# Latent attention in a 16-head kernel: the query product and its rotation issued behind all three score groups of a head

## What is computed

```python
qc = rms_norm(x @ wq_down, q_norm_w)                  # 96 columns
q_nope = (qc @ wq_up).reshape(bs, seq_len, H, DN)     # 16 heads
q_pe = apply_rope((qc @ wq_rope).reshape(bs, seq_len, H, DR), cos, sin)
kvc = rms_norm(x @ wkv_down, kv_norm_w)               # 64 columns
scores = jnp.einsum('bqhd,bkhd->bhqk', q, k) * scale  # causal mask
probs = softmax(scores + mask)
out = jnp.einsum('bhqk,bkhd->bqhd', probs, v).reshape(bs, seq_len, H * DV)
return out @ wo
```

## Time and profile before

| what | value |
|---|---|
| three runs | 1478.59, 1483.33, 1485.69 us; median 1483.33 |
| the profiled execution, its own time | 1489.86 us |
| its span in the trace | 1487.8 us |
| TensorE busy | 1288.7 us (87%) |
| VectorE busy | 949.1 us (64%) |
| ScalarE busy | 672.6 us (45%) |
| GpSimd busy | 493.0 us (33%) |
| mean granted TensorE clock | 0.945 of full speed |

### The profile page before, as it was taken

The page is one execution under the profiler, slowest core; times in us unless marked ns, Lnnn a source line. Parts: engine busy times, 40 slices in busy tenths (PEclk is TensorE's granted clock), DMA queues, the critical chain, the costliest instruction groups (busy, mean ns, idle before and its releaser), DMA issues.

```text
span 1487.8 us, 22532 instructions
## 1 busy us (share of the span) xinstructions
PE 1288.7 (87%) x6702; PEld 831.9 (56%) x6702; DVE 949.1 (64%) x2798; ACT 672.6 (45%) x1706; POOL 493.0 (33%) x495
## 2 busy tenths in 40 slices
PE   6769898898887599998769889889889997899997
PEld 4514243343335588887536455556556555778886
DVE  6786758777778322224598878887897793033334
ACT  2205655565672055553245444554554452255550
POOL 2054040052214455551211211351143143355551
PEclk7959998999999799999998999999999998899999
DMA  8627543074304276544010000020010112255647
GB/s 284 107 27 114 184 85 43 1 147 152 146 25 159 96 240 196 189 153 143 15 43 29 29 1 1 11 103 1 8 37 15 58 36 100 94 198 180 207 136 300
DMA packets 78928, 152.15 MB, mean 102 GB/s; under 512 B 11677, under 2 KB 60254, under 8 KB 75230
## 3 DMA queue, kind: packets, MB, share of 16 engines
q1 hardware_dynamic: 63022, 108.59, 25.5%
q0 software_dynamic: 15360, 41.96, 7.9%
q10 hardware_dynamic: 432, 0.17, 0.0%
HBM read 85.29 MB, written 65.01 MB: 101 GB/s over the span
## 4 chain that ended last, share of the span: by engine, by line
PE 56%; DVE 28%; ACT 6%; issue 6%; DMA 3%; POOL 1%; SPq 0%; DVEq 0%; POOLq 0%; ACTq 0%
PE m_psG L1263 12%; PE m_psY L1279 5%; DVE a_t L1713 5%; DVE a_mx L914 4%; PE a_psA L1472 3%; DVE a_nb L1721 3%; PE a_psO L478 3%; PE m_psX L1254 3%; PE a_psU L1454 3%; PE a_psU L453 3%; ACT a_pr L1583 2%; PE m_psY L161 2%; PE a_psO L1495 2%; PE a_psW L419 2%; PE a_psP L1485 2%
## 5 line engine op out<-in xcount | busy, mean ns | idle before, releaser
L166 POOL DMA_INDIRECT outs_dram<-m_ys,dest x192 | 183.9, 958 | 166.4 <-ACT m_ys L1184 152.5
L1583 ACT ACTIVATE a_pr<-a_psA,a_nb 128x512 f32<-128x512 f32 (+3 forms) x256 | 132.6, 524 | 220.2 <-DVE a_nb L1721 219.3
L1204 DVE TENSOR_TENSOR m_hm<-m_psG,m_sg 128x128 f32<-128x128 f32 x192 | 56.0, 292 | 270.1 <-ACT m_sg L1178 171.2
L1263 PE MATMUL m_psG<-arena,m_xgT 128*128 x768 | 203.6, 388 | 3.9 <-ACT m_xgT L1172 2.7
L914 DVE TENSOR_REDUCE a_mx<-a_psU 128x1 f32<-128x512 f32 x256 | 163.6, 684 | 67.5 <-PE a_psU L453 61.7
L1639 POOL TENSOR_TENSOR a_q<-a_q,a_t 64x512 f32<-64x512 f32 x64 | 80.8, 1263 | 356.5 <-DVEq L1716 336.1
L166 POOL DMA_INDIRECT rows_dram<-a_xd,slot x112 | 115.0, 1027 | 157.0 <-DVE a_xd L146 74.5
L602 ACT ACTIVATE a_P<-a_psS 128x512 f32<-128x512 f32 x256 | 142.8, 597 | 51.1 <-PE a_psS L464 44.9
L1263 PEld LDWEIGHTS m_psG<-arena,m_xgT 128*128 128x128 f32 x768 | 131.6, 191 | 20.8 <-issue 9.2
L1721 DVE TENSOR_REDUCE a_nb<-a_psA 128x1 f32<-128x512 f32 (+3 forms) x256 | 113.3, 485 | 38.1 <-PE a_psA L1474 28.5
L453 PE MATMUL a_psU<-arena 96*128 96x512 bf16 x256 | 106.1, 416 | 33.2 <-DVE a_mx L914 31.2
(11 more groups left out here) (296 smaller groups left out, 2377.4 us busy)
## 6 DMA issues: line engine op xcount, KB each, us to landing
m_xg<-rows_dram SPq DMA_DIRECT2D x46, 512.0 KB
arena<-in_mo_w SPq DMA_DIRECT2D x9, 2048.0 KB
arena<-part_dram SPq DMA_DIRECT2D x96, 128.0 KB
arena<-outs_dram SPq DMA_DIRECT2D x18, 512.0 KB, 3.9
rows_dram<-a_P SPq DMA_DIRECT2D x6, 1024.0 KB, 14.2
part_dram<-a_part SPq DMA_DIRECT2D x16, 384.0 KB, 5.4
rows_dram<-arena SPq DMA_DIRECT2D x6, 1024.0 KB, 15.0
arena<-outs_dram SPq DMA_DIRECT2D x5, 1024.0 KB, 11.1
```

Of the source, the lines that this page charges most:

```text
L166: pool.indirect_dma_start(out=rows_dram, out_offset=bass.IndirectOffsetOnAxis(ap=slot[:, c:c + 1], axis=0), in_=row, in_offset=None).then_ ...
L1263: ins = pe.matmul(psG[b % 2][:, 0:2 * INTER], xgT[:, (b % 2) * D + k * P:(b % 2) * D + (k + 1) * P], GU[:, ds(e * (KD * 2 * INTER) + k * 2 ...
L1583: ins = act.activation(pr[S % 2][:, AT[t]:AT[t] + (t + 1) * P], psA[:, AT[t]:AT[t] + (t + 1) * P], ACT.Exp, bias=nb[S % 2][:, t:t + 1], sc ...
```

## The change

Two loops are reordered and nothing else. TensorE issues all three groups of scores of head S and then the query product of head S + 2. VectorE takes all three groups of maxima and then rotates that query. The unit order in `psU`, the semaphores, the other engines' lists and all shapes stay.

```diff
@@ TensorE, step S @@
                 if S < HEADS:
-                    scores(S, 0)
+                    for k in range(NBK):
+                        scores(S, k)
                     if S + 2 < HEADS:
                         queries(S + 2)
-                    for k in range(1, NBK):
-                        scores(S, k)
                 if S >= 3 and S % 2:
                     values((S - 3) // 2)
@@ VectorE, step S @@
-                maxima(S, 0)
+                for k in range(NBK):
+                    maxima(S, k)
                 if S + 2 < HEADS:
                     queries(S + 2)
-                for k in range(1, NBK):
-                    maxima(S, k)
                 for k in range(NBK):
                     divide(S, k)
```

## The result

The changed kernel takes 1543.05 us (median of 4 runs, 1541.75 to 1548.56) beside 1484.51 us for the kernel before on the same chip: 1.0392 times, with a 95% interval of 1.0363 to 1.0422, so **58.5 us slower**. The forecast was 1526, with 1507 to 1547 as its range.

A forecast was written before the change was run, and what follows sets the result against it. VectorE and TensorE were both taken as near full, each pacing some latent-stage steps. Step costs, less 2.9 us of returns, plus 3.4 for the clock, summed to +42.4 us on 1483.3: 1525.7, say 1526, range 1507 to 1547.

The forecast's parts named there:

- the clock rival: Longer pauses before every side unit put TensorE's half clock on further steps: about 1543, up to 1555 us; chance 0.14.
- signs of being wrong: First division product near 0.5, steps without side unit at 5.87 or less, or steps growing with clock well below 0.96.
- The collision: GpSimd's addition holds VectorE's first division product: 0.91 us lost, net +0.69 a VectorE-paced step, 12.4 over 18 steps.
- the savings: On VectorE, taking the maxima together removes gaps and overlaps the rest: 0.22 us saved in a VectorE-paced step.
- Steps entered with TensorE last: Seven steps ended by VectorE, where the query product now comes later on TensorE: +1.28 us each, 9.0 in all.
- Steps 14, 16, 32 and 48: These four steps were counted at 4.0 us in the sum.
- Scatter steps: Nine steps where stores make GpSimd late: -0.22 to +0.69 us each, taken as 0.45, 4.0 in all.
- Even output products: TensorE's output products wait for the later rotation: 4.5 us (20, 36, 52), 3.2 (18, 34, 50), clock 3.4 (34, 50).
- Steps 9, 25 and 40: Steps 9 and 25 at +0.3 us, step 40 at +1.0: 1.6 in all.
- The returns from earlier exponentials: Earlier ScalarE exponentials give back time in steps 13 (-1.5), 15 (-0.75), 31 and 47 (-0.3): -2.9 us in all.
- no collision: GpSimd's addition starts late enough to slip between VectorE's products: +9.1 us, 1492; chance 0.12.
- earlier exponentials free TensorE: TensorE's 21.9 us of score waits on ScalarE go, with the collision absent: 1461 us; chance 0.04.

The follow-up runs named there:

- the filler run: The full change plus 12 filler products of 128x128 on TensorE ahead of every side unit of an even step: 1526.36 us, 1.0265 times the kernel before.
- the collision alone: The kernel before, order untouched, but GpSimd's addition waits for the last maximum so that it starts with the division: 1504.55 us, 1.0188.
- the run without most of the collisions: The full change, with GpSimd's addition waiting for the next head's first maximum except in steps that also scatter rows: 1510.52 us, 1.0162.
- the 18 chosen steps: The kernel before, with the new order and GpSimd's addition behind the next first maximum only in 18 VectorE-paced steps: 1484.72 us, 1.0000.

## Why the prediction was right, and what it missed

The direction and the main cause were right, and the time is inside the range. It is 17 us above the forecast, though, and on the very number of the clock rival (about 1543); one of my own signs of being wrong came as well, the clock row at 0.91, well below 0.96. That the range reached to 1547 is what covers this. Measured 58.5 us against 42.4: the terms, summed over the steps of the two traces (56.1 us there):

- *The collision.* Worked out: product ends 0.28 behind the addition, +0.69 a VectorE-paced step, 6.56. Measured: 0.29, +0.79 in the plain ones, 6.64 to 6.66, and the 18 steps named together 13.5 for 12.4. The step of the working that was short is the hand-over from the last product of the division to the first maximum of the next step: I let it start 0.08 before the product's end, as in the old order, and it starts 0.03 behind it (1009.67 in step 33 without the collision, where the product ends at 1009.64). So the savings were 0.13 instead of 0.22, and that step takes 5.74, not 5.65. Why the overlap is gone I have not found.
- *Steps entered with TensorE last:* 1.30 to 1.86 each for 1.28; 10.2 for 9.0. Steps 14, 16, 32 and 48: 4.5 for 4.0. Step 0: 1.1 for 2.2. Even key steps: 1.7 for 1.0.
- *Scatter steps:* 6.9 for 4.0, of which step 29 alone 2.9.
- *Even output products:* 14.6 for 11.1, clock included. I left step 20 at full clock (10.3); it took 12.14. Steps 36 and 52 did come at 10.45.
- *Steps 9, 25 and 40:* 4.1 for 1.6.
- *The returns from earlier exponentials* are **the term that failed**: -2.9 was counted, -0.6 came (13: 0.0, 15: -0.2, 31: -0.2, 47: -0.2). The exponentials did come earlier, but steps 13 and 15 lost the gain again: 13 takes 8.10, with a granted clock of 0.79, 6.67 with the fillers, and 6.44 with the addition beside the next maxima, where 15 takes 6.45 for 7.35. So those two gains were there, 2.5 us for the 2.25 I gave them, in a kernel without the collision; I had counted them in a kernel with it.

So what was under-sized is the clock, in the terms for side units and returns: counted at 3.4, it carries up to the 19 us of the filler run. I had priced it as a rival of its own, on top of the collision. The runs show the two mixed: with the addition beside the next maxima the clock is back at 0.95 and fillers win next to nothing; with the addition behind the division it stays at 0.92 though plain steps are as short (5.72); and the collision alone, in the old order, leaves it at 0.96. So, as far as these runs go, the low clock came with the longer pauses of the new order, and the collision made some of these longer still. Of the Trainium skill's rules, that of "SBUF — State Buffer", section "Who interferes with whom", agrees with all runs: the products wait for the whole of the addition, the reductions of step 33 don't. What the Trainium skill says in "TensorE: Matmul & The Clock Gate", section "HAM oscillation — how this bites in real kernels", is about pauses longer than the 2.15 us here, so I stretched it when I had it say that steps 20, 36 and 52 would be slow; the trace has one of the three slow.

The rival "no collision" falls by the mean of 1261 ns. The rival "earlier exponentials free TensorE" falls by the run without most of the collisions: even there the new order is 1.016.

Open: which pauses cost the clock. Steps 36 and 52 kept it where step 20 lost it with the same wait ahead; the six output products waited 15.8 us in all with the addition behind the division and 14.9 beside the next maxima, and four were slow in the first and one, that of step 18, in the second. Open too is why the 18 chosen steps gave no gain in the whole time.

## What to carry to other kernels

Before an operation is moved on VectorE, look at what its end releases on GpSimd, and what VectorE will be doing then: here an in-place product with a scalar from SBUF to SBUF stood until GpSimd's addition was done (1.41 us for 0.49), and a reduction out of PSUM beside the same addition did not. A wait that was hidden (ScalarE's 219 us) was no gain to be had. And where two engines share a hand-written order, half of a reordering can be slower than the whole, so test by costs (a wait that moves one operation) rather than by halves.

## What the runs showed that I had not expected

- GpSimd needs only 0.06 us of lead to hold a product for its whole 1.27 us: 1.49 us for 0.49.
- The same conflict stretches additions of two SBUF tensors with a scalar: 2.92 us for 2.04 for four.
- Moving GpSimd's addition beside the next maxima raised TensorE's granted clock over the steps from 0.91 to 0.95 with no change to TensorE's list; moving it behind the division raised it only to 0.92.
- The clock fell inside the output product and not in the pause ahead of it (step 20).
- Fillers of 2.68 us ahead of a unit that waited 2.15 still gained 1.4 in step 20, and the same fillers in the kernel before cost 1.9 in the same step.
